# Transformer block with mixture of experts on one core: output bias moved into the projection's bank, six subtractions moved from VectorE to GpSimd

## What is computed

```python
x = x + attention(layernorm(x))          # 16 heads of 16, causal, softmax
    qkv = xn @ W_qkv + b_qkv
    attn = softmax(mask(q @ k.T * scale))
    out = (attn @ v) @ W_out + b_out     # b_out: the bias this case is about
x = x + ffn(layernorm(x))                # 8 experts, hidden 1024, top 2
    xn = layernorm(layernorm(x)) * gamma + beta
    w, idx = top_k(softmax(xn @ gate_w), 2), normalised
    output = sum over the 2 experts of w * (gelu(xn @ w1 + b1) @ w2 + b2)
    ffn = output + its input
```

## Time and profile before

| | |
|---|---|
| median of 3 runs | 971.87 us (971.49 to 972.29) |
| the profiled execution, whole | 968.22 us |
| its span (first to last instruction) | 966.4 us |
| TensorE busy in the span | 838.2 us, 87% |
| VectorE busy | 706.9 us, 73% |
| ScalarE busy | 573.4 us, 59% |
| GpSimd busy | 483.6 us, 50% |
| TensorE's granted clock, mean | 0.915 |

### The profile page before, as it was taken

One profiled execution on the slowest core, in us unless ns is written; L12 is line 12 of the kernel. 1 busy time (PEld: TensorE's weight loads), 2 busy tenths in 40 slices (PEclk: granted clock), 3 DMA queues, 4 the chain that ended last, 5 costly groups with the idle time before them and its releaser, 6 DMA issues.

```text
span 966.4 us, 20943 instructions
## 1 busy us (share of the span) xinstructions
PE 838.2 (87%) x6728; PEld 554.0 (57%) x6728; DVE 706.9 (73%) x1566; ACT 573.4 (59%) x1048; POOL 483.6 (50%) x574
## 2 busy tenths in 40 slices
PE   4899967878787888787688699998999999999996
PEld 2555422332343424242242488887888888888875
DVE  6677878868669797987968278784676766666664
ACT  1767456655768777876958475463554445445453
POOL 4000023324545666757476846785568464554441
PEclk9999978877889879887986799999999999999999
DMA  9888657745767658566743985536435444444331
GB/s 203 258 263 280 233 162 222 214 113 156 196 199 205 188 155 227 136 179 175 193 122 84 269 131 101 82 53 137 68 58 95 84 75 71 79 74 83 56 69 23
DMA packets 184950, 139.39 MB, mean 144 GB/s; under 512 B 97968, under 2 KB 167472, under 8 KB 184720
## 3 DMA queue, kind: packets, MB, share of 16 engines
q1 hardware_dynamic: 154272, 96.82, 39.3%
q0 software_dynamic: 15680, 18.95, 12.4%
q10 hardware_dynamic: 14896, 22.28, 7.1%
HBM read 83.63 MB, written 44.80 MB: 133 GB/s over the span
## 4 chain that ended last, share of the span: by engine, by line
PE 44%; DMA 17%; DVE 11%; POOL 11%; SPq 7%; issue 6%; ACT 3%; POOLq 0%; ACTq 0%; DVEq 0%
PE banks L769 16%; PE banks L787 15%; PE banks L593 5%; POOL slot_tokens L1652 4%; DMA arena<-in_L_attn_x 3%; DMA weighed_values<-arena 3%; DMA arena<-arena 3%; DMA inverse_sums<-arena 2%; PE banks L696 2%; PE banks L583 2%; SPq L1788 2%; DVE weights L1383 2%; SPq L1786 2%; POOL out L1705 2%; POOL arena L1722 1%
## 5 line engine op out<-in xcount | busy, mean ns | idle before, releaser
L979 ACT ACTIVATE arena<-banks,arena 128x256 f32<-128x256 f32 (+1 forms) x312 | 152.6, 541 | 183.4 <-issue 89.5
L769 PE MATMUL banks<-arena,weights 128*128 128x256 f16 (+1 forms) x1872 | 206.2, 267 | 9.4 <-DMA arena<-arena 8.8
L769 PEld LDWEIGHTS banks<-arena,weights 128*128 x1872 | 175.2, 99 | 35.9 <-issue 11.6
L787 PE MATMUL banks<-weights,arena 128*128 x1704 | 194.0, 273 | 0.8 <-DVE arena L1513 0.8
L1705 POOL DMA_INDIRECT out<-arena x71 | 115.9, 1633 | 141.7 <-DVE arena L1524 92.5
L787 PEld LDWEIGHTS banks<-weights,arena 128*128 128x128 f16 x1704 | 164.9, 98 | 23.0 <-issue 2.2
L652 PE MATMUL banks<-arena 64*128 64x128 f16 (+3 forms) x512 | 121.5, 339 | 40.3 <-DMA arena<-arena 13.6
L1511 DVE TENSOR_SCALAR arena<-arena 128x512 f16<-128x512 f32 (+1 forms) x156 | 77.6, 498 | 71.3 <-ACT arena L979 69.4
L624 PE MATMUL banks<-arena 62*128 62x384 f16 (+3 forms) x512 | 98.5, 333 | 30.2 <-DVE arena L1218 11.3
L1513 DVE SCALAR_TENSOR_TENSOR arena<-arena 128x512 f16<-128x512 f32 (+1 forms) x156 | 111.1, 712 | 5.6
L652 PEld LDWEIGHTS banks<-arena 64*128 64x128 f16 x512 | 38.7, 100 | 128.4 <-issue 37.8
(11 more groups left out here) (191 smaller groups left out, 1267.7 us busy)
## 6 DMA issues: line engine op xcount, KB each, us to landing
weights<-in_L_ffn_w ACTq DMA_DIRECT2D x16, 1024.0 KB, 7.6
arena<-in_L_ffn_w SPq DMA_DIRECT2D x32, 512.0 KB
qk_parts<-weights SPq DMA_DIRECT2D x64, 128.0 KB
arena<-qk_parts SPq DMA_DIRECT2D x128, 64.0 KB, 3.5
weighed_values<-arena SPq DMA_DIRECT2D x32, 256.0 KB, 4.0
token_rows<-arena SPq DMA_DIRECT2D x12, 512.0 KB, 4.3
arena<-qk_parts SPq DMA_DIRECT2D x128, 32.0 KB, 3.6
arena<-weighed_values SPq DMA_DIRECT2D x32, 128.0 KB
```

Source lines behind the costliest of these rows:

```text
L769: m = pe.matmul(bank[:, c * TILE:c * TILE + WIDTH[j]], w1[:, k, wp, f:f + P], xp[:, k, 0:WIDTH[j]], start=(i == 0), stop=(i == len(terms) ...
L787: m = pe.matmul(bank[:, c * D:(c + 1) * D], hp[:, f, c * P:(c + 1) * P], w2[:, f // (FC // 2), wp, f % (FC // 2), :], start=(f == 0 and i ...
L979: m = act.activation(h_32[r % 2][:, c, 0:WIDTH[j]], banks[:, 1 + c2, c * TILE:c * TILE + WIDTH[j]], ACT.Gelu, bias=b1_now[j % 2][:, 2 * c2 ...
```

## The change

1. `with_bias` is gone. `b_out` is split into three bfloat16 parts (GpSimd, once, in the prologue), which three small DMAs lay into rows 0 to 2 of a 128 x 256 tile whose other rows are zero. A third matmul in each group of `out_proj` multiplies a tile of ones with it, so that the bank holds the projection and the bias: four more matmuls of 128 x 256 a batch.
2. `add_out` waits for `load_again`'s DMA itself (`x_again`) instead of for `with_bias`.
3. `row_low` of batches 0 to 5 is issued by GpSimd; batches 6 and 7 stay on VectorE.
4. The first numbers made by GpSimd's iota lie in `rows` in place of `b_out`, and the exponentials of the first two units wait for the bias parts, whose source lies where they write.

```diff
@@ the table
             at(base + 166, "load_again", b)
-            at(base + 186, "with_bias", b)
@@ TensorE
                 w.wait_ge(sem("vectors_in"), 96)
+                w.wait_ge(sem("bias_parts_in"), 48)
                 bank = take_side("out_proj", (b, half))
                 for s in range(2):
                     tt = 2 * half + s
+                    out = bank[:, s * D:(s + 1) * D]
                     for k in range(KC):
-                        m = pe.matmul(bank[:, s * D:(s + 1) * D], o_inverse[k][:, tt * P:(tt + 1) * P], w_out[:, k, :],
-                                      start=(k == 0), stop=(k == KC - 1))
+                        pe.matmul(out, o_inverse[k][:, tt * P:(tt + 1) * P], w_out[:, k, :], start=(k == 0), stop=False)
+                    m = pe.matmul(out, ones_b, b_out, start=False, stop=True)
@@ VectorE
             def add_out(b, half):
-                w.wait_ge(sem("with_bias"), b + 1)
+                w.wait_ge(sem("x_again"), 16 * (b + 1))
...
-                elif stage == "row_low":
+                elif stage == "row_low" and n >= B - 2:
                     split_rows(n)
@@ GpSimd, prologue
+            w.wait_ge(sem("vectors_in"), 96)
+            m = own.mark(g.tensor_copy(bias_part[0], bias_all))
+            w.wait_ge(own.sem, m)
+            m = own.mark(g.tensor_tensor(bias_rest[0], bias_all, bias_part[0], ALU.subtract))
+            w.wait_ge(own.sem, m)
+            m = own.mark(g.tensor_copy(bias_part[1], bias_rest[0]))
...
+            for i in range(3):
+                g.dma_start(b_out[i:i + 1, :], bias_part[i][i:i + 1, :]).then_inc(sem("bias_parts_in"), 16)
@@ GpSimd, timetable
-                elif stage == "with_bias":
-                    w.wait_ge(sem("x_again"), 16 * (n + 1))
-                    w.wait_ge(sem("vectors_in"), 96)
-                    g.tensor_tensor(rows, rows, over_tiles(b_out), ALU.add).then_inc(sem("with_bias"), 1)
...
+                elif stage == "row_low" and n < B - 2:
+                    w.wait_ge(sem("row_high"), n + 1)
+                    g.tensor_tensor(row_low, rows, row_high, ALU.subtract).then_inc(sem("row_low"), 1)
```

More of the change, by code:

```diff
@@ L141, in build @@
         banks = ctx.enter_context(nc.psum_tensor("banks", [P, 8, 512], F32))
-        keep = Area(arena, 0, 3088 + 2 * TT)
+        keep = Area(arena, 0, 3088 + 2 * TT - D // 2)
         ident = keep.take(P)
@@ L152, in build @@
         beta = keep.take(D)
-        b_out = keep.take(D)
+        b_out = keep.take(D // 2, BF16)
         w_out = keep.take(KC * D, k=KC, n=D)
@@ L206, in build @@
         rows = a2.take(TT * D, t=TT, d=D)
+        scratch = rows[:, 0, :]
         row_high, row_low = (x2[:, :, i * D // 2:(i + 1) * D // 2].bitcast(F16) for i in range(2))
@@ L272, in build @@
         weighed_b2 = [a5.take(TC * D, c=TC, d=D) for _ in range(2)]
+        bias_all = p_T[1][:, 0, 0:D]
+        bias_rest = [p_T[1][:, 0, (1 + i) * D:(2 + i) * D] for i in range(2)]
+        bias_part = [p_T[1][:, 0, 3 * D + i * D // 2:3 * D + (i + 1) * D // 2].bitcast(BF16) for i in range(3)]
         w_sb = weights[:, :].rearrange("p (e w) -> p e w", e=E)
@@ L1063, in numbers @@
                 w.wait_ge(sem("consts"), 1)
-                v.tensor_copy(iota_16, b_out[:, 0:P].bitcast(I32))
+                v.tensor_copy(iota_16, scratch[:, 0:P].bitcast(I32))
                 v.memset(running, 0.0)
-                v.tensor_copy(prefer, b_out[:, P:P + E].bitcast(I32)).then_inc(sem("numbers"), 1)
+                v.tensor_copy(prefer, scratch[:, P:P + E].bitcast(I32)).then_inc(sem("numbers"), 1)
             def rsqrt_step(step, s, y_, u_):
@@ L1600, in gpsimd @@
             own.mark(g.memset(ones_b, 1.0))
+            own.mark(g.memset(b_out, 0.0))
             own.mark(g.memset(minus_half, -0.5))
@@ L1611, in gpsimd @@
                             channel_multiplier=-1)
-            g.iota(b_out[:, 0:P].bitcast(I32), [[1, P]], base=0, channel_multiplier=0)
-            g.iota(b_out[:, P:P + E].bitcast(I32), [[-1, E]], base=E, channel_multiplier=0)
+            g.iota(scratch[:, 0:P].bitcast(I32), [[1, P]], base=0, channel_multiplier=0)
+            g.iota(scratch[:, P:P + E].bitcast(I32), [[-1, E]], base=E, channel_multiplier=0)
             g.iota(spare_row, [[0, LOCAL]], base=N, channel_multiplier=1)
@@ L1622, in gpsimd @@
             m.then_inc(sem("memory_set"), 1)
+            w.wait_ge(sem("vectors_in"), 96)
[4 more added lines that the diff above has]
+            m = own.mark(g.tensor_copy(bias_part[1], bias_rest[0]))
+            w.wait_ge(own.sem, m)
+            m = own.mark(g.tensor_tensor(bias_rest[1], bias_rest[0], bias_part[1], ALU.subtract))
+            w.wait_ge(own.sem, m)
+            m = own.mark(g.tensor_copy(bias_part[2], bias_rest[1]))
+            w.wait_ge(own.sem, m)
+            for i in range(3):
+                g.dma_start(b_out[i:i + 1, :], bias_part[i][i:i + 1, :]).then_inc(sem("bias_parts_in"), 16)
             w.wait_ge(sem("tops"), 2 * 2 * LATE)
@@ L1753, in sync @@
             sp.dma_start(beta, rows_of(t["L0_ffn_beta"])).then_inc(sem("vectors_in"), 16)
-            sp.dma_start(b_out, rows_of(t["L0_attn_b_out"])).then_inc(sem("vectors_in"), 16)
+            sp.dma_start(bias_all, rows_of(t["L0_attn_b_out"])).then_inc(sem("vectors_in"), 16)
             sp.dma_start(w_out, t["L0_attn_W_out"].rearrange("(k p) n -> p k n", p=P)).then_inc(sem("vectors_in"), 16)
```

## The result

The changed kernel takes 956.54 us (median of 4 runs, 955.56 to 958.36) where the kernel before takes 971.68 us (970.27 to 972.29): a ratio of 0.9848, with a 95% interval of 0.9829 to 0.9868. The forecast was 968.4 us with a range of 961 to 976. So the sign was right and the size was not: 15.1 us came where 3.5 were summed, and even the rival "deeper gain" (960.7) was too small.

A forecast was written before the change was run, and what follows sets the result against it. The prediction took attention to be bound by waits passing between engines, none full, and the expert stage by TensorE. Its terms, -4.4 - 1.2 + 0.3 + 2.5 + 1.0 - 1.7 = -3.5 us, took 971.87 to 968.4 us, range 961 to 976.

The forecast's parts named there:

- deeper gain: Rival, attention: all five TensorE waits for masks behind the removed addition go; -11.2 us in all, 960.7 us; chance 0.16.
- with_bias goes: Attention, GpSimd: without the addition and its wait for x, masks come earlier and TensorE waits less; -4.4 us.
- The two cancel: GpSimd's list before the mask: added row_low (2.36 us) offsets the removed addition, leaving only the idle time ahead as gain.
- The smaller of lead and TensorE's wait: Batches 2 to 5: TensorE gains the lesser of GpSimd's idle time before the addition and its mask wait; 6.7 us together.
- Of 6.7 I take two thirds: Attention: the summed mask gain of 6.7 us is cut to 4.4, since other waits meet some of it.
- Batch 0: First batch's attention: add_out starts 2.36 us earlier and TensorE's 1.21 us wait for a VectorE reduction goes; -1.2 us.
- add_out against a later x: Three attention batches: row_low on GpSimd ends later, delaying rows_out and the x reload, so add_out waits longer; +0.3 us.
- VectorE's relief: Attention: VectorE loses six subtractions, 8.5 us of its work, but soon waits anyway; 0 us (0 to -3).
- The added matmuls: Output projection on TensorE: four more bias matmuls in each of eight batches; +2.5 us (0.4 to 9.6).
- The handover: Attention to experts: row_low of batch 5 on GpSimd delays the gather that starts the first expert tile; +1.0 us.
- batch 7: Last batch, GpSimd: the addition's 2.36 us go, and with them TensorE's 1.74 us wait for the divide; -1.7 us.
- The slower rival: Rival, attention: SyncE's queue, held at rows_out for GpSimd's row_low, delays loads in three batches; 976.8 us; chance 0.22.

The follow-up runs named there:

- the two kernels in which VectorE still waits for the addition: Kernel before with only row_low of batches 0 to 5 moved to GpSimd: 1.0068; kernel before with the addition one place later in GpSimd's list: 0.9988.
- the run made for it: Changed kernel with row_low of batch 5 put back on VectorE: ratio 0.9872 to the kernel before.

## Why the forecast was wrong

**The step that failed** is the first term, *with_bias goes*: -4.4 us by my sum for batches 2 to 5. Some 3 us of work put back at that place in these four batches cost 8.5 us (0.9924 against 0.9837), and in all eight 12.7. The mechanism was the right one and its price was too low. Of the three cuts that made the price, the first is shown to be wrong.

- *"The two cancel."* I let `row_low` pay for the addition's 2.36 us and counted only the idling ahead of it as a lead. Between `row_low` and that mask GpSimd waits for VectorE before the first store of `place`, 2.71 us in batch 4, and that takes up part of it. The masks came 2.9, 2.3, 3.6 and 5.9 us ahead where I had 3.15, 0, 1.71 and 3.17. The run with the bias alone and the one with both are equal, so the move was free in this list. Batch 3 is the plainest case: 0 forecast, 2.4 measured.
- *"The smaller of lead and TensorE's wait."* Behind the late mask GpSimd also has `root`, for which VectorE waits 6.7 us in batches 2 to 5. I read TensorE's waits and `add_out`'s, and not who else waits for what stands later in GpSimd's list. The deeper-gain rival named root operations, and I gave it 0.16. What `root` is worth stays open: the four units gain 13.0 us where TensorE waited 8.9 for masks, but with the units between them it is 7.7, and no run moved `root` alone.
- *"Of 6.7 I take two thirds."* The discount stood on a mean, 90 us of waits in the stage, and on no row. It is not shown to be wrong: between 215 and 530 us TensorE's waits for masks, 9.6 us, went, and those for VectorE's reduction L1231 (L1224 before) rose from 6.3 to 11.0.

**The clock** had no term in the sum; I wrote that it was worth a few us either way. About 4 of the 15.1 us go with it, by the estimate above, so a part of the miss is not the mechanism's.

**Batch 0**, -1.2: the path was right and the size too small. The unit with the wait is 3.2 us shorter, and the two kernels in which VectorE still waits for the addition don't have that.

**add_out against a later x**, +0.3: `add_out`'s waits are 6.5 us in three places, less than before. The forecast's direction was wrong for the total; it was small.

**VectorE's relief**, 0: right. The bias alone does as well as both. The rule of the Trainium skill (GPSIMD Engine Reference, Elementwise — side-by-side cycle accounting), by which the move costs the difference of the engines, gave +5.7 us for the move by itself; the run that made only the move has +6.6 (2.8 to 10.3 us, from its interval). That agrees with what it would do to the kernel before. With the addition gone the same move costs nothing, so in the whole change it was no term. The estimate of 2.2 us for the operation agrees with the 2.30 us that the trace gives as a mean of six, five of them at 2.12 to 2.14 and one at 3.12. Part of the relief was also taken back: in batches 3 to 5 one small operation of VectorE beside `row_low` takes 1.98 to 2.10 us (rows in the last section).

**The added matmuls**, +2.5: not visible; without them the kernel is no faster, within some 6 us. Their rows have 9.2 us of busy time for 32; that TensorE had gaps for them is a reading and not shown.

```profile
L715 PE MATMUL banks<-arena 128*128 128x256 bf16 x32 | 9.2, 287 | 0.0
```

**The handover**, +1.0, **and batch 7**, -1.7: neither is left in the end. The first did not show in the run made for it; the second wait went, and the next one grew by 1.5 us.

**The slower rival** decided by the slack of SyncE's queue, and the queue had it: the loads cost TensorE 3.6 us more in all. Its mechanism did appear when the gather was moved alone.

## What to carry to other kernels

When an in-order engine's instruction goes, follow its list to the next place where that engine would idle anyway, and read every engine that waits for something in between; the one with the longest wait need not be the only one that pays. An instruction that is moved in ahead doesn't cancel one that is taken out unless no wait lies between the two. The same 3 us cost 2.1 us at one place in the list and nothing that can be measured at another some ten instructions ahead, so the price belongs to the place and not to the operation.

## What the runs showed of the hardware

GpSimd and VectorE can hold each other up although they work on different data. `row_low` on GpSimd (L1755) and small operations of VectorE over 8 elements, in the changed kernel:

```profile
365.69 2.14 POOL L1755 TENSOR_TENSOR arena<-arena 128x1024 f16<-128x1024 f32 x1
365.88 1.98 DVE L1376 TENSOR_SCALAR arena<-arena 128x8 int32<-128x8 int32 x1
...
475.09 2.14 POOL L1755 TENSOR_TENSOR arena<-arena 128x1024 f16<-128x1024 f32 x1
475.27 1.99 DVE L1376 TENSOR_SCALAR arena<-arena 128x8 int32<-128x8 int32 x1
```

```profile
310.82 0.17 DVE L1376 TENSOR_SCALAR arena<-arena 128x8 int32<-128x8 int32 x1
```

The same operation takes 0.17 us where GpSimd is idle and 2 us where it starts beside `row_low`, and then it ends within 0.05 us of GpSimd's end. In batch 4 both sides show it: VectorE runs a two-input operation over 1024 elements until 420.35, and `row_low` beside it takes 3.12 us in place of 2.14; VectorE's next one, over 8 elements, takes 2.10 us and ends with it.

```profile
418.83 1.52 DVE L1390 SCALAR_TENSOR_TENSOR weights<-arena,weights 128x1024 f16<-128x1024 f32 x1
420.27 2.10 DVE L1373 SCALAR_TENSOR_TENSOR arena<-arena 128x8 f32<-128x8 f32 x1
```

The ratio may depend on the chip: the kernel before took from 972 to 992 us on the chips used, and the changed kernel's relatives with little or no wait for GpSimd lay at 0.986 to 0.988 on one slow chip and at 0.990 to 0.991 on the other, with intervals of about 0.003 to 0.006 to either side.
